# Nine columns instead of twelve in the twelfth unit of each edge pass, and the first pass's flags and weights prepared one trip later

## The reference

```python
_segment_sum = lambda x, seg: jax.ops.segment_sum(x, seg, num_segments=3125)
x = _layernorm(x + gin0(x))      # mlp(x + _segment_sum(x[src], dst)), batch norm, relu
x = _layernorm(x + gin1(x))      # mlp(x + _segment_sum(x[src], dst))
h = x @ enc_W + enc_b            # message layers
for l in range(3):
    cat = jnp.concatenate([h[src], h[dst], edge_attr], axis=-1)
    m = relu(cat @ msg_W1[l] + msg_b1[l]) @ msg_W2[l] + msg_b2[l]
    h = gru_cell(_segment_sum(m, dst), h)
x = _layernorm(x + relu(h @ ro_W1 + ro_b1) @ ro_W2 + ro_b2)
x = _layernorm(x + gat(gat(x)))  # softmax over the edges of a node, twice
```

## Time and profile before

| what | value |
|---|---|
| time, median of 3 runs (lowest to highest) | 3002.78 us (3001.18 to 3006.99) |
| time of the profiled execution | 3005.72 us |
| its span in the trace | 3003.6 us |
| PE busy | 2627.3 us, 87% of the span |
| POOL busy (without the issue time between two gathers) | 2114.1 us, 70% |
| DVE busy | 2036.7 us, 68% |
| ACT busy | 1493.3 us, 50% |
| chain that ended last | PE 77%, DVE 8%, ACT 5%, issue 4%, POOL 3%, DMA 2% |

### The profile page before, as it was taken

The page is one execution under the profiler, slowest core; times in us unless marked ns, Lnnn a source line. Parts: engine busy times, 40 slices in busy tenths (PEclk is TensorE's granted clock), DMA queues, the critical chain, the costliest instruction groups (busy, mean ns, idle before and its releaser), DMA issues.

```text
span 3003.6 us, 75122 instructions
## 1 busy us (share of the span) xinstructions
PE 2627.3 (87%) x28348; PEld 2437.8 (81%) x28348; DVE 2036.7 (68%) x7400; ACT 1493.3 (50%) x2632; POOL 2114.1 (70%) x2178
## 2 busy tenths in 40 slices
PE   7999668999799999589998599995899995799981
PEld 6999648999569999269998289994499995699981
DVE  6988744555447999558999669998445555455565
ACT  7777438888344444144443344442634443344443
POOL 6777637677657777577777577776567776777774
PEclk9999858999799999699999799997799997799995
DMA  5666718999538999359998289995288785488872
GB/s 171 216 226 215 204 48 271 360 363 320 152 115 280 307 311 302 103 177 310 306 306 263 77 276 305 308 312 168 39 249 259 254 260 190 107 263 254 260 222 46
DMA packets 321474, 688.75 MB, mean 229 GB/s; under 512 B 114939, under 2 KB 150245, under 8 KB 302708
## 3 DMA queue, kind: packets, MB, share of 16 engines
q1 hardware_dynamic: 227584, 537.99, 53.4%
q0 software_dynamic: 69344, 70.04, 11.1%
q10 hardware_dynamic: 24340, 78.40, 6.7%
HBM read 487.50 MB, written 198.70 MB: 228 GB/s over the span
## 4 chain that ended last, share of the span: by engine, by line
PE 77%; DVE 8%; ACT 5%; issue 4%; POOL 3%; DMA 2%; SPq 1%; DVEq 0%; ACTq 0%; POOLq 0%
PE ps L1771 68%; PE ps L1723 4%; DVE ringG L1229 2%; ACT big L915 2%; POOL ringG L796 2%; PE ps L1732 2%; POOL nodes L796 1%; ACT big L970 1%; DVE edge_side L1229 1%; PE ps L1792 1%; PE ps L1689 1%; DVE ringG L1283 1%; DVE ringG L1333 1%; ACT ringG L935 1%; DMA big<-first_d 0%
## 5 line engine op out<-in xcount | busy, mean ns | idle before, releaser
L1771 PE MATMUL ps<-big 128*128 128x192 bf16 (+1 forms) x25275 | 2255.9, 247 | 1.7 <-issue 1.7
L1771 PEld LDWEIGHTS ps<-big 128*128 128x128 fp8e4 (+1 forms) x25275 | 2132.6, 98 | 43.9 <-issue 5.2
L796 POOL DMA_INDIRECT ringG<-tab,src_i x1596 | 1537.4, 963 | 528.4 <-issue 469.3
L1229 DVE SCALAR_TENSOR_TENSOR ringG<-ringG,same 128x64 f32<-128x64 f32 x2075 | 584.9, 282 | 89.7 <-ACT ringG L924 33.3
L915 ACT ACTIVATE big<-src_hot,node_minus 128x1536 fp8e4<-128x1536 int16 x242 | 369.0, 1573 | 144.2 <-PE ps L1771 113.9
L915 ACT ACTIVATE big<-big,node_minus 128x1536 fp8e4<-128x1536 int16 x239 | 364.4, 1573 | 134.1 <-PE ps L1771 127.1
L1229 DVE SCALAR_TENSOR_TENSOR edge_side<-edge_side,same 128x64 f32<-128x64 f32 x1245 | 349.5, 281 | 17.1
L1333 DVE SCALAR_TENSOR_TENSOR ringG<-ringG,expo 128x65 f32<-128x65 f32 x830 | 238.9, 288 | 156.3 <-ACT ringG L935 79.3
L796 POOL DMA_INDIRECT ringG<-in_x,src_i x266 | 270.0, 1015 | 105.7 <-issue 82.9
L924 ACT ACTIVATE ringG<-ringG 128x512 f32<-128x512 f32 x156 | 98.4, 631 | 426.8 <-DVE ringG L1283 426.8
L882 ACT COPY big<-ps 128x384 f32<-128x384 f32 (+1 forms) x450 | 208.0, 480 | 184.3 <-PE ps L1771 183.0
(11 more groups left out here) (269 smaller groups left out, 1773.0 us busy)
## 6 DMA issues: line engine op xcount, KB each, us to landing
big<-kept SPq DMA_DIRECT2D x117, 1152.0 KB
big<-kept SPq DMA_DIRECT2D x78, 960.0 KB
sums<-ringG SPq DMA_DIRECT2D x260, 256.0 KB
kept<-big ACTq DMA_DIRECT2D x91, 576.0 KB
edge_side<-q_at_start SPq DMA_DIRECT2D x156, 256.0 KB
big<-kept SPq DMA_DIRECT2D x26, 1344.0 KB
big<-kept SPq DMA_DIRECT2D x52, 576.0 KB
big<-kept SPq DMA_DIRECT2D x39, 768.0 KB
```

What stands on the lines that cost most here:

```text
L796: return pool.indirect_dma_start(out=out_ap, out_offset=None, in_=table, in_offset=bass.IndirectOffsetOnAxis(ap=index, axis=0))
L1229: return v.scalar_tensor_tensor(now, before if u == 0 else source[:, (u - 1) * D:u * D], same[:, c:c + 1], now, ALU.mult, ALU.add)
L1771: mm = pe.matmul(ps[:, b, 0:2 * n] if wide else ps[:, b, to:to + n], hot[t][0:rows, u * P:(u + 1) * P], opener[:, 0:2 * n] if wide else sp ...
```

## The change

A third kind of unit, `NEAR = (0, 3, 3, 3)`, stands in trip 11 of every pass: nine hot columns in five banks, none in the trip's first group, which POOL gathers whole. So `unit.first` is 1 there, DVE takes the products after g44, and ACT's copies of this unit are no longer made at the end of trip 10 but in trip 11, behind g44's clip or weigh. `way.before(i)` counts the banks of the units before trip i. In pass 0, DVE's flags and weights move behind trip 10, the first transpose on PE into the middle of unit 11, and the second between units 11 and 12. In the first attention pass SP issues the second piece of one-hot tiles after the last rows of the tables and no longer before them.

```diff
+        return self.last if i == TRIPS - 1 else self.near if i == TRIPS - 2 else self.most
+    def before(self, i):
+        return sum(self.unit(n).banks for n in range(i))
...
-HOT, LAST = Hot((3, 3, 3, 3)), Hot((0, 0, 3, 3))
+HOT, NEAR, LAST = Hot((3, 3, 3, 3)), Hot((0, 3, 3, 3)), Hot((0, 0, 3, 3))
...
@@ SP, tables of the first attention pass
-                    if l == 0 and c == NC - 2:
-                        sp.wait_ge(*FILL("l2_back", NC - 1))
-                        feed_piece(5, 0, 1)
                 if l == 0:
-                    for q in range(2, len(TILES)):
+                    for q in range(1, len(TILES)):
                         feed_piece(5, 0, q)
...
@@ ACT, act_pass
                         elif 2 <= k < 5:
-                            if j == GROUPS - 1 and i + 1 < TRIPS - bool(PASSES[k].last.first):
+                            if j == GROUPS - 1 and i + 1 < TRIPS and not PASSES[k].unit(i + 1).first:
                                 evict(k, i + 1, range(EARLY_BANKS))
                             clip(k - 2, g)
                         elif k >= 5:
                             weigh(k - 5, g)
-                        if PASSES[k].last.first and i >= TRIPS - 2:
-                            if i == TRIPS - 1 and j == PASSES[k].last.first - 1:
-                                evict(k, i)
-                        elif j == GROUPS - 1 and i + 1 < TRIPS:
+                        if j == PASSES[k].unit(i).first - 1:
+                            evict(k, i)
+                        elif j == GROUPS - 1 and i + 1 < TRIPS and not PASSES[k].unit(i + 1).first:
                             evict(k, i + 1, range(EARLY_BANKS if 2 <= k < 5 else 0, banks))
...
@@ DVE, pass 0
             v.scalar_tensor_tensor(first[:], edge_row[:], float(L), count[:], ALU.mult, ALU.add
                                    ).then_inc(first_ready, 1)
+            pooled_trip(0, 10)
+
             v.wait_ge(pens_turned, 1)
             link(v.tensor_copy(pen_row[:, 0:P], ps[0:1, 7, 0:P]))
             v.tensor_scalar(last_row[:], pen_row[:, 1:P + 1], -1.0, None, ALU.is_lt).then_inc(lasts_ready, 1)
-            v.wait_ge(lasts_turned, 1)
-            link(v.tensor_copy(last_of[:], ps[:, 7, 0:1]))
...
-            pooled_trip(0, 10)
+            v.wait_ge(lasts_turned, 1)
+            v.tensor_copy(last_of[:], ps[:, 7, 0:1]).then_inc(lasts_read, 1)
...
@@ PE, pass 0 (the other passes take way.near in trip 11 and LAST in trip 12)
-            pe.wait_ge(rows_used, NT)
-            pe.wait_ge(pens_ready, 1)
-            pe.transpose(ps[0:1, 7, 0:P], flag[:, 4:5], ident[:]).then_inc(pens_turned, 1)
+            for q in range(len(TILES)):
+                fetch_piece(0, trip_of(TRIPS - 2), q, PASSES[0].near)
+                if q == 1:
+                    pe.wait_ge(rows_used, NT)
+                    pe.wait_ge(pens_ready, 1)
+                    pe.transpose(ps[0:1, 7, 0:P], flag[:, 4:5], ident[:]).then_inc(pens_turned, 1)
             pe.wait_ge(lasts_ready, 1)
             pe.transpose(ps[:, 7, 0:1], last_row[:], ones[0:1, :]).then_inc(lasts_turned, 1)
-            fetch_unit(0, trip_of(TRIPS - 2))
-            fetch_unit(0, trip_of(TRIPS - 1), last=True)
+            fetch_unit(0, trip_of(TRIPS - 1), LAST)
             pe.wait_ge(weights_in, 16 * len(weight_loads))
+            pe.wait_ge(lasts_read, 1)
```

More of the change, by code:

```diff
@@ L210 @@
 STEP, TOP, PEAK = 4194304.0, 1024.0, 32.0
-PASSES = ([Pass(0, HOT, LAST), Pass(1, HOT, LAST)] + [Pass(2 + l, HOT, LAST) for l in range(NLAYER)]
-          + [Pass(5 + l, HOT, LAST, WG) for l in range(2)])
-BANKS_BEFORE = [sum((TRIPS - 1) * w.banks + w.last.banks for w in PASSES[:k]) for k in range(len(PASSES) + 1)]
+NEARS = [NEAR, NEAR, NEAR, NEAR, NEAR, NEAR, NEAR]
+PASSES = [Pass(k, HOT, NEARS[k], LAST, D if k < 5 else WG) for k in range(7)]
+BANKS_BEFORE = [sum(w.before(TRIPS) for w in PASSES[:k]) for k in range(len(PASSES) + 1)]
 GATHERED = []
@@ L308, in build @@
         ringG = sb("ringG", [P, RING, COLS * WG])
-        cold_max = max(unit.cold(j) for way in PASSES[2:5] for unit in (way.most, way.last) for j in range(GROUPS))
+        cold_max = max(unit.cold(j) for way in PASSES[2:5] for unit in (way.most, way.near, way.last) for j in range(GROUPS))
         edge_side = sb("edge_side", [P, QRING * COLS * D + ERING * cold_max * P // 2])
@@ L1207, in take_products @@
                 got = way.fetched
-                v.wait_ge(evicted, OPEN + BANKS_BEFORE[k] + i * way.banks + unit.banks)
+                v.wait_ge(evicted, OPEN + BANKS_BEFORE[k] + way.before(i + 1))
                 link(by_pieces(unit.u // 3, unit.u, lambda n: v.tensor_tensor(
@@ L1739, in settle, with fetch_piece @@
                 pe.sem_inc(unit_open, 1)
-            def fetch_piece(k, at, q, first=False, last=False):
-                way, unit = PASSES[k], PASSES[k].last if last else PASSES[k].most
+            def fetch_piece(k, at, q, unit, first=False):
+                way = PASSES[k]
                 split, n = split_of(way), 3 * way.fetched
@@ L1780, in trip_of, with fetch_unit @@
                 return lambda times, plus: i * times + plus
-            def fetch_unit(k, at, first=False, last=False):
+            def fetch_unit(k, at, unit, first=False):
                 for q in range(len(TILES)):
-                    fetch_piece(k, at, q, first, last)
+                    fetch_piece(k, at, q, unit, first)
             def edge_products(l, s, bank, loaded, added, columns):
@@ L1866, in _ @@
             run_wave("gin0_end", {"l0_back": node_product(FM[1][0:D], centre[:], D)})
-            fetch_unit(1, trip_of(0), True)
-            with pe.Fori(1, TRIPS - 1) as i:
-                fetch_unit(1, trip_of(i))
-            fetch_unit(1, trip_of(TRIPS - 1), last=True)
+            fetch_unit(1, trip_of(0), HOT, True)
+            with pe.Fori(1, TRIPS - 2) as i:
+                fetch_unit(1, trip_of(i), HOT)
+            fetch_unit(1, trip_of(TRIPS - 2), PASSES[1].near)
+            fetch_unit(1, trip_of(TRIPS - 1), LAST)
             pe.wait_ge(summed, 2 * NG)
@@ L1899, in _ @@
                 k = 5 + l
-                fetch_unit(k, trip_of(0), True)
-                with pe.Fori(1, TRIPS - 1) as i:
-                    fetch_unit(k, trip_of(i))
-                fetch_unit(k, trip_of(TRIPS - 1), last=True)
+                fetch_unit(k, trip_of(0), HOT, True)
+                with pe.Fori(1, TRIPS - 2) as i:
+                    fetch_unit(k, trip_of(i), HOT)
+                fetch_unit(k, trip_of(TRIPS - 2), PASSES[k].near)
+                fetch_unit(k, trip_of(TRIPS - 1), LAST)
                 pe.wait_ge(maxima_ready, l + 1)
```

33 lines of the change are left out of this document (16 added, 17 removed).

## The result

The changed kernel takes **3009.87 us** (median of 15 runs, 3004.07 to 3012.69) against 3002.19 us of the kernel before beside it (15 runs, 2998.35 to 3006.99): ratio 1.0023, 95% interval 1.0016 to 1.0029. It is 7.7 us slower; 9.2 us less were forecast. The profiled execution took 3008.6 us, with a span of 3006.8.

The account below looks back on a forecast made before the run. PE paces until unit 10 or 11, then read-back, gathers or DVE bound the pass ends. Minus 10 (pass 0), plus 3.8 (1), minus 3.4 (2 to 4), minus 3.0 (5), plus 3.4 (6): minus 9.2, 2993.6 us, range 2988 to 2999.5.

Parts of the forecast that it names:

- Then g40's store, the read-back and L1502 come 10.4 us earlier: Pass 0: with flags, weights (6.2 us) and a 4.26 us wait gone from before g40, L1502 comes at 342.6.
- SP reads `first` back only behind the store of g40: Pass 0: the read-back waits for g40's store (333.92, then 14.69 us of transfer); DVE waits for it until 353.06.
- the stated bounds of 6.6 to 10.4: Pass 0's gain: 6.6 us if all POOL stalls stay, 10.4 if the read-back decides; 10 was taken.
- The first rival: Pass 0 gives half: POOL's stalls and DVE's waits stay or the read-back stalls, minus 5 us, 2998.6; chance 0.17.
- the 4.26 us gone: Trip 10 of pass 0: DVE's idle wait for PE's first piece of unit 11 goes, as unit 11 follows the row products.
- 342.6 or 344.7 were worked out: Pass 0: L1502 at 342.6 by the earlier read-back; DVE there at 344.7 by its own work, a gain of 8.4 us.
- the idle time ahead of g47 gone: Pass 0: POOL's 10.39 us idle before g47, waiting for g40, which DVE has late, was to disappear.
- PE's two new waits: Pass 0: PE waits for last-row flags ahead of unit 12 and `last_of` behind it; only unit 12 and small products follow.
- where 7 were taken: Pass 5: gathers begin 7 us earlier, between 9.8 and not at all, as the last `adtab` write precedes the one-hot tiles.
- The third rival: The gathers of pass 5 begin no earlier; pass 5 loses 0.6 us instead of gaining 3.0, 2997.2; chance 0.10.
- the room of 4.8 us: End of pass 4: the last gather lands 4.8 us before DVE wants it at 2092.53; three more gathers cost 3.8.
- the second rival: The gathers become the bound in every pass; passes 1 to 6 lose 3.8 us each, 3015.6, slower; chance 0.07.

Follow-up runs that it names:

- the unit alone: Kernel before with only the nine-column unit in all seven passes, pass 0 in its old order and pass 5's one-hot piece where it was: 3003.95 us, ratio 1.0009.
- the order alone: Kernel before with only pass 0's new order, twelve columns and pass 5's one-hot piece fed where it was: 3002.47 us, ratio 1.0002.
- in the old order with everything mended: Full change with `first` stored as rows, `nxt` copied in SBUF, zeros earlier, twelve columns in passes 1 and 6, pass 0's old order: 2990.09 us, ratio 0.9949.

## Why the prediction was wrong

From the end of one pass to the end of the next, over all fourteen traces (mean; lowest to highest):

| pass | twelve columns | nine columns | difference | forecast |
|---|---|---|---|---|
| 0 (kernel before, full change) | 385.4 | 385.8 | +0.4 | -10 |
| 1 (7 and 7 traces) | 414.7 (412.5 to 416.6) | 419.0 (418.1 to 420.4) | +4.3 | +3.8 |
| 2 (4 and 10) | 447.6 (446.4 to 448.1) | 447.3 (446.1 to 448.9) | -0.3 | -1.2 |
| 3 (4 and 10) | 428.7 (427.3 to 430.3) | 427.7 (426.6 to 429.1) | -1.0 | -1.2 |
| 4 (4 and 10) | 420.9 (419.7 to 423.7) | 419.5 (418.0 to 421.4) | -1.4 | -1.0 |
| 5 (4 and 10) | 441.8 (440.9 to 442.3) | 438.6 (437.3 to 440.4) | -3.2 | -3.0 |
| 6 (7 and 7) | 410.5 (410.0 to 411.1) | 413.5 (412.4 to 414.7) | +3.0 | +3.4 |

The sum is +1.8 against a forecast of -9.2. Of the 11.0 us between them 10.4 are pass 0.

- **The step that failed** is "Then g40's store, the read-back and L1502 come 10.4 us earlier". It rested on "SP reads `first` back only behind the store of g40". SP waits there for two things, and the prediction priced the one that it saw last. In the kernel before both were over by 333.50. The read begins, and so the store of `first` has landed, 16.3 to 18.6 us behind the issue of that store, at 331.3 to 334.6, in the eight traces in which SP stands waiting for it. In the kernel before that would be 331.2 to 333.5. So moving g40 could give about 2 us at most, where 10.4 were taken. No gain at all lay outside the stated bounds of 6.6 to 10.4; POOL and DVE were checked as the next bound, the store of `first` was not. The first rival did name a stall of the read-back, but let it take half of the gain; it took the whole.
- **What took these 2 us back, and the unit's shorter read:** ACT's stores, which came 15 us earlier and into the read. With the unit alone some 5.5 MB moved during the read-back (323 GB/s over 17.1 us), in the full change some 7.7 (336 over 23); six stores of zeros and a piece of one-hot tiles are 2.1. Taking the zeros out shortened the read by 3.7 us of the 5.7 by which it is longer than with the unit alone (22.8 against 17.1); the other 2 are open.
- **Right in pass 0:** the flags' copy behind trip 10, the 4.26 us gone, DVE at the masks early (340.9, and 342.6 or 344.7 were worked out), the idle time ahead of g47 gone, PE's two new waits harmless. That DVE was early took the shorter pieces of unit 11 as well: with the order alone it came at 351.3.
- **Right:** passes 1 and 6, where the gathers are the bound and three of them cost 4.3 and 3.0; pass 5; and pass 3, though its ranges overlap. In pass 5 the gathers begin 5.8 us sooner, where 7 were taken. Over all traces it is 4.3 (97.1 us behind the end of pass 4 without the move, 92.8 with it). The third rival, that they would not, is out.
- **Half right:** passes 2 and 4. Behind the first sum pass 2 is 1.2 us shorter in the mean (326.1 against 327.3), as worked out, but the stage in front of it varies by more than that. In pass 4 the room of 4.8 us was not enough: in seven of ten traces with nine columns DVE waits 1.5 to 4.0 us for a gather some 17 us before the end, 4.00 in the full change, and in none of the four with twelve. PE begins 57.2 to 59.6 us behind the end of pass 3 there and POOL 69.9 to 70.9; an early PE alone does not decide it, since at 57.7 one trace shows 4.03 us and another none. There the second rival, the gathers as the bound, is half true; not in passes 2 and 3.
- **Open:** the profiled stages give +1.8, the medians +2.9 on one chip and +7.7 on another. Nothing in the traces shows where the rest lies; the end of the read-back, and the stages between passes that no edit touches, vary by 2 to 3 us from one execution to the next (masks at 354.1, 354.3 and 356.8 in three kernels with the same pass 0).

## What to carry to other kernels

An instruction that waits for two things shows only the one that came last, and the list of waits can miss even that; the pauses in the queue's timeline are the surer sign. Before pricing a step moved out of its way, look up when the other was ready; a store that is read back is one of the two, and its own landing is the floor. Engines that get free earlier issue their stores earlier: look what these fall into. And a unit that trades matmuls for gathers is to be set pass by pass, since here it costs where POOL comes last (passes 1 and 6) and gains clearly only in pass 5.

## What was not expected of the hardware

A store of 12.5 KB took 16.3 to 18.6 us to land when it was written as 3,200 elements of 4 bytes (from 315.03 to 331.28 in one trace, 314.55 to 333.12 in another), with all DMA engines busy at 37 GB/s, and it slowed others: a copy of 127 rows of 100 bytes issued behind it needed 10.54 us for its issue alone (7.39 with the same copies in the kernel before), 0.82 behind the store of 25 rows. The two forms of the latter, in SP's queue, first behind the element store, then behind the row store:

```profile
320.70 10.54 SPq L711 DMA_DIRECT2D nxt<-first  x1
```

```profile
317.13 0.82 SPq L713 DMA_DIRECT2D nxt<-first  x1
```

Two broadcasts of 1.6 MB each into 128 partitions took 15 to 17 us beside the kernel's other transfers (333.01 to 349.81 with ACT's zeros among them, 329.89 to 345.27 without, in the old order with everything mended).
